# A transformer block with self and cross attention on one core: start-up memsets moved, the VectorE order of a pair of batches rearranged, cross queries ahead of the cross outputs

## What is computed

```
mod = silu(cond) @ W_mod + b_mod            # shift_a, scale_a, gate_a, shift_m, scale_m, gate_m
q, k, v = modulate(LN(x), shift_a, scale_a) @ W_qkv + b_qkv
x = x + gate_a * (softmax(q k' * 8**-0.5) v @ W_proj + b_proj)
q_c = LN(x) @ W_qc + b_qc ;  k_c, v_c = LN(context) @ W_kvc + b_kvc
x = x + (softmax(q_c k_c' * 8**-0.5) v_c @ W_cproj + b_cproj)
x = x + gate_m * (gelu(modulate(LN(x), shift_m, scale_m) @ W_mlp1 + b_mlp1) @ W_mlp2 + b_mlp2)
```

## Time and profile before

| | |
|---|---|
| median of 3 runs | 415.6 us (414.44, 415.6, 418.48) |
| the profiled execution | 415.69 us, its span 413.5 us |
| slots 4 to 13 (the loop) | about 95 to 270 us |
| slots 14 to 19 | about 270 to 345 us |
| MLP alone | from about 345 us |
| busy share of the span | PE 81%, ACT 66%, DVE 65%, POOL 46% |

### The profile page before, as it was taken

The page is one execution under the profiler, slowest core; times in us unless marked ns, Lnnn a source line. Parts: engine busy times, 40 slices in busy tenths (PEclk is TensorE's granted clock), DMA queues, the critical chain, the costliest instruction groups (busy, mean ns, idle before and its releaser), DMA issues.

```text
span 413.5 us, 15982 instructions
## 1 busy us (share of the span) xinstructions
PE 336.2 (81%) x5880; PEld 230.2 (56%) x5880; DVE 269.7 (65%) x682; ACT 272.3 (66%) x523; POOL 189.9 (46%) x462
## 2 busy tenths in 40 slices
PE   3455776978798898988989889899786487999994
PEld 2333454656676666766667666676554354445442
DVE  7764666868778788787888878877645350534311
ACT  1134563868688787787877888777682457577572
POOL 6523354756456565665656557555352310211200
PEclk9997998999999999999999999999998988999998
DMA  5323388243242523425243261433330300000101
GB/s 149 76 75 82 94 196 188 61 102 93 70 111 64 141 63 93 100 68 141 54 102 91 68 150 44 113 93 74 77 72 12 80 2 2 25 27 25 51 25 51
DMA packets 65548, 33.13 MB, mean 80 GB/s; under 512 B 8359, under 2 KB 65255, under 8 KB 65511
## 3 DMA queue, kind: packets, MB, share of 16 engines
q1 hardware_dynamic: 63599, 32.56, 32.3%
q10 hardware_dynamic: 1912, 0.07, 0.3%
HBM read 4.83 MB, written 2.10 MB: 17 GB/s over the span
## 4 chain that ended last, share of the span: by engine, by line
PE 40%; DVE 23%; issue 13%; SPq 10%; DMA 5%; ACT 3%; ACTq 2%; POOL 2%; DVEq 1%; POOLq 0%
SPq L406 7%; PE ps_o L1178 7%; PE wide L1170 7%; PE wide L1109 5%; PE ps_o L1131 5%; DVE mx L734 4%; DMA qkc_st<-qkcp 4%; DVE mxc L734 4%; DVE x_n L712 3%; PE ps_misc L1206 3%; PE wide L1120 2%; SPq L411 2%; DVE qkr L751 2%; PE ps_misc L1219 2%; DVE x_stats L696 2%
## 5 line engine op out<-in xcount | busy, mean ns | idle before, releaser
L734 DVE TENSOR_REDUCE mx<-wide 128x8 f32<-128x1024 f32 x64 | 78.0, 1219 | 26.4 <-PE wide L1109 26.4
L902 ACT ACTIVATE p_c<-wide 128x1024 f32<-128x1024 f32 x64 | 65.5, 1023 | 30.7 <-PE wide L1120 30.3
L902 ACT ACTIVATE p_s<-wide 128x1024 f32<-128x1024 f32 x64 | 65.5, 1023 | 19.7 <-PE wide L1120 19.0
L734 DVE TENSOR_REDUCE mxc<-wide 128x8 f32<-128x616 f32 x64 | 50.5, 789 | 21.7 <-PE wide L1109 21.7
L1131 PE MATMUL ps_o<-p_c,vc_m 128*32 128x128 f32 x1024 | 43.8, 292 | 0.3 <-ACT s_sum L923 0.2
L1131 PE MATMUL ps_o<-p_s,v_m 128*32 128x128 f32 x1024 | 42.5, 285 | 0.0
L523 POOL TENSOR_TENSOR x_ve<-x_mv,eps_sb 128x2 f32<-128x2 f32 x32 | 6.2, 195 | 76.5 <-DVE x_mv L703 76.5
L1109 PE MATMUL wide<-qkc_st 62*128 62x77 bf16 x512 | 20.5, 203 | 21.8 <-DMA qkc_st<-qkcp 11.3
L1109 PEld LDWEIGHTS wide<-qkc_st 62*128 62x128 bf16 x512 | 12.2, 98 | 36.4 <-DVE mxc L734 18.3
L1109 PE MATMUL wide<-qk_st 62*128 62x128 bf16 x512 | 26.0, 223 | 5.6 <-DVE mx L734 4.1
L1170 PE MATMUL wide<-m_nT,w_sb 128*128 128x512 f32 x64 | 30.0, 603 | 0.2 <-DVE mxc L734 0.2
(11 more groups left out here) (153 smaller groups left out, 811.8 us busy)
## 6 DMA issues: line engine op xcount, KB each, us to landing
qk_st<-qkp SPq DMA_DIRECT2D x96, 128.0 KB, 2.6
qkc_st<-qkcp SPq DMA_DIRECT2D x96, 128.0 KB, 2.5
out<-m_out SPq DMA_DIRECT2D x8, 256.0 KB, 2.3
xs<-x SPq DMA_DIRECT2D x3, 512.0 KB, 4.3
qk_st<-nmT SPq DMA_DIRECT2D x64, 4.0 KB
qkc_st<-nmcT SPq DMA_DIRECT2D x64, 4.0 KB
ctx_sb<-ctx SPq DMA_DIRECT2D x3, 308.0 KB
w_sb<-L_xcond_W_mlp SPq DMA_DIRECT2D x2, 256.0 KB, 4.8
```

The costliest lines, as they stand in the source:

```text
L734: nc.vector.reduce_max(mxt[:, b].rearrange("q (x r) -> q r x", r=2)[:, r], src, AX.X, negate=True).then_inc(sems[done], 1)
L902: nc.scalar.activation(dst[u % 2][:].rearrange("k x q -> k (x q)"), ps_st[:].rearrange("k s x -> k (s x)"), ACT.Exp, scale=SCALE).then_inc ...
```

## The change

Seven edits, none of which changes what is computed:

1. Start: the condition vector has a semaphore of its own (`cond_in`), so its transpose no longer waits for `w_mod`.
2. DVE's zeroing of `v_m` and the ones in it (`key_sums`) move from the head of the program and from beat 0 of slot -2 to the end of beat 5 of slot -2.
3. POOL's zeroing and ones of `qkc_st` and the zeroing of `qkcp` move from the end of slot -1 to the end of slot -2, behind a wait for `x_n_set`.
4. DVE: the two remainders `qkr` are apart: queries at beat 2 as before, keys at beat 3, after that beat's maxima. The statistics of the context move from beat 5 to beat 1, those of x1 from beat 4 to beat 5, the normalising of x from beat 6 to beat 5, and that of x1 at beat 6 from before the maxima to after them.
5. POOL: `split_max` of batch 1 of h comes before the self parts (`halves`) of a.
6. PE: `q_c` comes before `obc_t` at beat 7; `q_c` takes bank 0 and `obc_t` bank 1.
7. ACT: the copy `qcx` moves from beat 0 of the next slot, after `ocT`, to the end of beat 7, after the exponential.

```diff
--- before.py
+++ after.py
@@ -89,7 +89,7 @@
         ("max_s1", "here", 0), ("proj", "back1", 2),
         ("kv_c", "back1", 1),
         ("max_c0", "back2", 0), ("oc_t", "back3", 1), ("x1_t", "back1", 2),
-        ("obc_t", "back3", 0), ("q_c", "back1", 1), ("x_t", "far", 2)]
+        ("q_c", "back1", 0), ("obc_t", "back3", 1), ("x_t", "far", 2)]
 BANK = {name: bank for name, _, bank in MISC}
 
 
...
@@ -387,7 +387,7 @@
                 lo, hi = PIECES[n:n + 2]
                 sp.dma_start(ctx_sb[:, lo:hi], ctx[lo:hi].rearrange("b t c -> t b c")).then_inc(sems[f"c_in{n}"], 16)
 
-            sp.dma_start(cond_sb[:], cond).then_inc(sems["wm_in"], 16)
+            sp.dma_start(cond_sb[:], cond).then_inc(sems["cond_in"], 16)
             sp.dma_start(wmod_sb[:], w_mod).then_inc(sems["wm_in"], 16)
             load_x(0)
             sp.dma_start(wqkv_sb[:], w_qkv).then_inc(sems["wq_in"], 16)
@@ -585,14 +585,14 @@
                     split_max(h, 0, mx, nm, "mx_set", "nmh_set", "nm_set", "mts_ps")
                 if d:
                     gated(d)
+                if h:
+                    split_max(h, 1, mx, nm, "mx_set", "nmh_set", "nm_set", "mts_ps")
                 if a:
                     if not a.first():
                         q = a.shift(-1)
                         w(pool, f"qk_in{q.par}", 16 * NCMB * (q.turn + 1))
                     hold(pool, "qkr_set", a.n + 1)
                     halves(a, qkr[:], [qkp[:, :, n] for n in range(3)], "qk")
-                if h:
-                    split_max(h, 1, mx, nm, "mx_set", "nmh_set", "nm_set", "mts_ps")
                 if d:
                     rstd("x1", d)
                 if f:
@@ -604,6 +604,15 @@
                           kcr[:].rearrange("c (b k) -> c b k", b=G), "kvc0_set", "kc", "qkc_in")
                 if f:
                     split_max(f, 1, mxc, nmc, "mxc_set", "nmch_set", "nmc_set", "mtc_ps")
+                if far and far.first():
+                    pool.wait_ge(sems["x_n_set"], 1)
+                    for par in range(2):
+                        nc.gpsimd.memset(qkc_st[par][:, :, 1].bitcast(u32), 0).then_inc(sems["z_pool"], 1)
+                    nc.gpsimd.memset(qkcp[:].bitcast(u32), 0).then_inc(sems["pad_set"], 1)
+                    pool.wait_ge(sems["z_pool"], 8)
+                    for par in range(2):
+                        nc.gpsimd.memset(qkc_st[par][:, :, 1].rearrange("c m (b k) -> c m b k", b=G)[:, :, :, 0:S],
+                                         1.0).then_inc(sems["zk_set"], 1)
                 if a and a.first():
                     pool.wait_ge(sems["wc_in"], 16 * 2)
                     for n, src in ((2, wqc_sb), (3, wkvc_sb)):
@@ -612,13 +621,6 @@
                                 wdh[:, n, HALF * s_:HALF * (s_ + 1)].rearrange("c (d m) -> c d m", d=D),
                                 src[:, 0:C].rearrange("c (m s d) -> c s d m", s=2, d=D)[:, s_])
                         last.then_inc(sems["wdc_set"], 1)
-                    for par in range(2):
-                        nc.gpsimd.memset(qkc_st[par][:, :, 1].bitcast(u32), 0).then_inc(sems["z_pool"], 1)
-                    nc.gpsimd.memset(qkcp[:].bitcast(u32), 0).then_inc(sems["pad_set"], 1)
-                    pool.wait_ge(sems["z_pool"], 8)
-                    for par in range(2):
-                        nc.gpsimd.memset(qkc_st[par][:, :, 1].rearrange("c m (b k) -> c m b k", b=G)[:, :, :, 0:S],
-                                         1.0).then_inc(sems["zk_set"], 1)
 
             slots(pool, slot)
 
@@ -631,9 +633,6 @@
 
             for st in qk_st:
                 nc.vector.memset(st[:, :, 0].bitcast(u32), 0).then_inc(sems["zq_set"], 1)
-            for vt in v_m:
-                nc.vector.memset(vt[:], 0.0).then_inc(sems["z_dve"], 1)
-
             dve.wait_ge(sems["cond_t"], 1)
             nc.vector.tensor_copy(condT[:], ps_max[:, 0, 0:B]).then_inc(sems["condT_set"], 1)
             dve.wait_ge(sems["tanh_set"], 1)
@@ -802,8 +801,6 @@
                         residual(z, "projc_ps", "proj_c", "x2_set")
                     if t == 3 and d:
                         attention_out(d, "s", "o_t", "ot_ps", "rden_set", "o_set", "obt_ps")
-                    if t == 6 and d:
-                        normalise("x1", d, x_of(d), "x1t_ps")
                     if t == 7 and e:
                         attention_out(e, "c", "oc_t", "oct_ps", "rdenc_set", "oc_set", "obct_ps")
 
@@ -819,7 +816,6 @@
                         stats("x", far, x_of(far))
                         aggregate("x", far)
                         if far.first():
-                            key_sums()
                             tables(range(2), 1)
                             head_columns()
                     if t == 2 and a:
@@ -827,23 +823,30 @@
                         if not a.first():
                             w(dve, "qk2_set", a.n)
                         rest(ps_misc[BANK["qk"]][:, 0:GT], bdh[:, 0:1], qkp[:, 0, 0], qkr[:, 0])
+                    if t == 3 and a:
                         rest(ps_misc[BANK["qk"]][:, GT:2 * GT], bdh[:, 1:2], qkp[:, 1, 0],
                              qkr[:, 1]).then_inc(sems["qkr_set"], 1)
                     if t == 4 and d:
                         residual(d, "proj_ps", "proj", "x1_set")
+                    if t == 5 and d:
                         hold(dve, "x1_set", d.n + 1)
                         stats("x1", d, x_of(d))
                         aggregate("x1", d)
-                    if t == 5 and h:
+                    if t == 1 and h:
                         arrived("c_in", h, {0: (0,), 1: (1,), 3: (2, 3, 4)})
                         stats("ctx", h, ctx_of(h))
                         aggregate("ctx", h)
-                    if t == 6 and far:
+                    if t == 5 and far:
                         normalise("x", far, x_of(far), "xt_ps")
                         if far.first():
                             tables(range(2, 6), 2)
                             for st in qkc_st:
                                 nc.vector.memset(st[:, :, 0].bitcast(u32), 0).then_inc(sems["zq_set"], 1)
+                            for vt in v_m:
+                                nc.vector.memset(vt[:], 0.0).then_inc(sems["z_dve"], 1)
+                            key_sums()
+                    if t == 6 and d:
+                        normalise("x1", d, x_of(d), "x1t_ps")
                     if t == 7 and h:
                         normalise("ctx", h, ctx_of(h), "ctxt_ps")
                 if a and a.first():
@@ -972,14 +975,6 @@
 
                     if t == 0 and z:
                         copy(ocT[:], ps_misc[BANK["obc_t"]][:, 0:GT], "obct_ps", z, "ocT_set", "projc_ps")
-                    if t == 0 and f:
-                        w(act, "qc_ps", f.n + 1)
-                        if f.first():
-                            act.wait_ge(sems["bc_in"], 16 * 4)
-                        else:
-                            w(act, "qcr_set", f.n)
-                        nc.scalar.activation(qcx[:], ps_misc[BANK["q_c"]][:, 0:GT], ACT.Identity,
-                                             bias=bdh[:, 2:3]).then_inc(sems["qc0_set"], 1)
                     if t == 1 and e:
                         empty_max(e, 1, "max_c1", "mtc_ps", nmcT, "nmcT_set", "mc_in")
                     if t == 1 and a:
@@ -1052,6 +1047,14 @@
                         values(v_m[a.par], T, ps_misc[BANK["v"]][:, 0:G * C]).then_inc(sems["v_set"], 1)
                     if t == 5 and e:
                         sums(e, "c", ps_o, "pvc_ps", "sumc_set", "oct_ps")
+                    if t == 7 and d:
+                        w(act, "qc_ps", d.n + 1)
+                        if d.first():
+                            act.wait_ge(sems["bc_in"], 16 * 4)
+                        else:
+                            w(act, "qcr_set", d.n)
+                        nc.scalar.activation(qcx[:], ps_misc[BANK["q_c"]][:, 0:GT], ACT.Identity,
+                                             bias=bdh[:, 2:3]).then_inc(sems["qc0_set"], 1)
 
                 if a and a.first():
                     for n in range(4):
@@ -1083,9 +1086,10 @@
             mm, tr = nc.tensor.matmul, nc.tensor.transpose
 
             pe.wait_ge(sems["id_set"], 1)
-            pe.wait_ge(sems["wm_in"], 16 * 2)
+            pe.wait_ge(sems["cond_in"], 16)
             tr(ps_max[:, 0, 0:B], cond_sb[:], ident[0:B, 0:B]).then_inc(sems["cond_t"], 1)
             pe.wait_ge(sems["silu_set"], 1)
+            pe.wait_ge(sems["wm_in"], 16)
             for k in range(6):
                 last = mm(ps_max[:, int(k < 2), k * B:(k + 1) * B], wmod_sb[:, k * C:(k + 1) * C], siluT[:], start=True, stop=True)
                 if k in (1, 5):
@@ -1362,10 +1366,10 @@
                         flip_sums("oc_t", "c", e, "sumc_set", "oct_ps")
                     if t == 6 and d:
                         transposed("x1_t", "x1", d, T, "x1t_ps")
+                    if t == 7 and d:
```

(5 more changed lines are left out.)

## The result

The changed kernel takes **426.1 us** (median; 424.05 to 429.33), the kernel before, on the same chip, 415.1 (414.44 to 418.48): a ratio of 1.021, 95% interval [1.016, 1.027]. The forecast was 418.8 with a range to 422.5, so it is slower than forecast by 7 us, and outside the range. The profiled execution took 425.76 us, with a span of 424.0 against 413.5.

What follows compares the result with a forecast made beforehand. A ring of DVE and PE bounds the loop, but the edits lengthen a second chain (L533, SP, `nmT`) to its limit. Terms -2.2 + 3.6 + 0.6 + 1.0 + 0.1 = +3.1 on 415.69 gave 418.8 us, range 413 to 422.5.

Steps and rivals of the forecast that it cites:

- +0.06 us a slot, +0.6 us for ten slots: Loop: what DVE's holes and the earlier cross queries give, the queue of L533, SP and `nmT` takes back.
- the walk of the keys' remainder: Loop: L533 starts 2.3 us later, so `nmT` lands at 215.8, 0.55 us late; next slot at 218.3 against 218.26.
- The edits of `qcx` and of the banks I cost at nothing: Cross queries: POOL takes `qcx` 0.4 us sooner but SP waits for `nmcT`; `q_c` waits for ACT's reading of `max_c0`.
- start: Before slot 0: L677 ends at about 20.3 instead of 22.78 without POOL's memsets; a gain of 2.2 us taken.
- slots 0 and 1: No room on the chain through L533: its delay counts fully, +1.5 us in slot 0 and +1.9 in slot 1.
- slots 2 and 3: Slot 2's x1 transposes, behind the third cross maxima, add 0.2 us; slot 3 adds nothing, its cross stack's landing ending last.
- slot 14: Old second chain with SP busy: +1.5 us if its 1.80 us gap stays, +0.3 if taken up; +1.0 taken.
- slot 15 to the end of the span: Slots 15 to 17: cross queries 0.4 us earlier, x1 transposes 0.5 later, +0.1; the MLP is not touched.
- The 19.0 that the prediction worked out for L677: Start: by the skill's shared-port rule L677 should have slipped in after the first memset, at about 19.0.
- the queue which I had taken for the limit: Loop: POOL's late L533, SP's stack issues and the landing of `nmT` end the slot, next slot at 218.3.
- The slower rival: Loop: POOL's `rstd` of x1 ahead of the first cross maxima's casts; 0.3 us more a slot, 421.8 us, chance 0.20.
- The other two rivals: Loop: queue has room, slot 17.1, 414.9 us, chance 0.20; DVE's holes filled fully, slot 16.9, 411.7 us, chance 0.15.

Runs made afterwards that it cites:

- the run with start and cross queries alone: Kernel before plus only the start edits and the cross queries ahead of the cross outputs, with their bank numbers: 17.08 us a slot, 411.9 us, ratio 0.984.
- the kernel with the keys back: Changed kernel with both halves of the remainders at beat 2 and POOL's second self-maxima casts behind the halves again: 17.36 us a slot, 416.4 us, ratio 0.999.
- the kernel before with x1 late: Kernel before with only x1's statistics behind the second cross maxima and its normalising behind the third: 17.74 us in most slots, 423.1 us, ratio 1.015.
- the run with other banks: Changed kernel with only bank numbers of small jobs changed (`qk` to 2, `ctx_t` to 1, among others): 17.42 us a slot, 422.0 us, ratio 1.009.

## Why the prediction was wrong

**The step that failed is the loop's "+0.06 us a slot, +0.6 us for ten slots"**; measured were 0.68 us a slot, +6.1 in all. In the walk of the keys' remainder I followed one of the two that wait for `qkr_set`, POOL's L533. The other one is PE's next job in bank 0, `ctx_t`; its wait was put at nothing, without a reason. Of banks the prediction asked only where `q_c` moves ("The edits of `qcx` and of the banks I cost at nothing", which held: the run with start and cross queries alone has them and got faster), and not who waits for a bank whose release comes later. By first maxima, against the forecast:

| stretch | forecast | measured |
|---|---|---|
| start (slot 0 begins at 25.83 instead of 27.84) | -2.2 | -2.0 |
| slots 0 and 1 | +3.4 | +4.7 |
| slots 2 and 3 | +0.2 | -0.5 |
| slots 4 to 13 | +0.6 | +6.1 |
| slot 14 | +1.0 | +0.7 |
| slot 15 to the end of the span | +0.1 | +1.5 |
| sum | +3.1 | +10.5 |

- *Start.* Right in size, and L677's instruction answered at once. The two x_n of pair 1, though, fared differently (view of the tile in that stretch: shortest, median and longest in ns):

```profile
L711 DVE TENSOR_SCALAR x_n<-xs,x_mv,x_rstd x2: 609/960/1312, 16.9 to 17.5; 128x128 f32<-128x128 f32 x2
```

  The first came through as L533 ended, at 17.5, as the 0.94 us of the earlier trace rows had let me assume for both. The second began within 0.1 us of L535 and ended at 18.78, 0.1 us after it. The Trainium skill (SBUF — State Buffer, Who interferes with whom) has whoever issues first keep the shared ports for the whole instruction. The first x_n agrees with that; for the second the two starts are too close to say; L677 before does not agree, since it was held over five memsets. The 19.0 that the prediction worked out for L677 by this rule is late besides: it was asked at 17.87, ahead of the first memset at 18.08.
- *Slots 0 and 1.* The mechanism was right, the size was not: they took 2.3 and 2.5 us more (18.09 and 18.01 against 15.82 and 15.54) for a forecast of 1.5 and 1.9. Against the kernel with the keys back it is 1.77 and 1.61, so 0.5 and 0.9 us are common to both (16.32 and 16.40 there). In slot 0 the edits did not bring them: the kernel before with x1 late, whose slot 0 is that of the kernel before, took 16.31. At its end the context's transposes and the next scores took PE 0.62 and 0.54 us, and 0.37 each in the kernel before. In slot 1 L533 began 9.0 us after the first maxima (52.92 against 43.92), where the forecast had 8.1 and the kernel before 6.2: the third maxima already came 4.5 us into it, 3.7 before. PE's granted clock over that slot was 0.97 in the changed kernel, 0.79 with the keys back and 1.00 before; what made it longer is not explained further.
- *Slots 2 and 3.* The forecast had the landing of a cross stack end last in both, the first one 1.2 us later than 68.45. In the changed kernel neither slot has a landing on its chain of waits; it runs through L533 and POOL instead, and the two slots took 0.5 us less than before, not 0.2 more.
- *The loop.* The changes add up slot by slot: cross queries -0.33 (17.41 to 17.08; the forecast had 0.45), x's normalising and the context's statistics early -0.08 (to 17.00), x1 late +0.36 (to 17.36), keys late +0.73 (to 18.09). The forecast had the gain of the first in it, about rightly; the last two were wrong or missing. Late keys cost 0.73 with x1 early or late (17.00 to 17.73, 17.36 to 18.09) and on the kernel before (17.41 to 18.14). With the bank out of the way 0.41 of it stays when x1 is early (17.00 to 17.41), and that is the queue which I had taken for the limit; the bank alone is then worth 0.32 (17.73 to 17.41), and 0.67 when x1 is late (18.09 to 17.42). Its walk was right to 0.1 us; it just was not what came last.
- *The slower rival* was at work (the row L1228 above), a slot of 17.36 by itself. It was priced at 0.3 us beyond the queue's limit, and measured 0.36 against a kernel that has no such limit. With the bank out of the way it and the late keys together gave 17.42, about the forecast's slot, and not 18.1. The other two rivals, under 17.2, fell with the first row of waits.
- *The end.* The drain and the MLP took 1.5 us more, 0.95 of it by the last cross maxima (334.81 - 287.06 = 47.75 us into the drain before, 344.76 - 296.06 = 48.70 now). The granted clock does not tell why: over the drain it is 0.93 in both (stretch, its length, PE's busy time with its instructions, granted clock, DMA share, GB/s; first before). The cause stays open.

```profile
287.06:335.60 48.54, 34.73 (x744) 0.93 0.22 52
```

```profile
296.06:345.60 49.54, 34.42 (x744) 0.93 0.22 51
```

The wait for the bank could be known beforehand. The list of jobs has `ctx_t` behind `qk` in bank 0, and `qkr_set` frees it. The transposes of the context fill columns 0 to 153 of the bank and the late half reads columns 256 to 511, so no data stand in each other's way; the program's semaphores guard whole banks, and whoever reads a bank late holds all of it. The Trainium skill (PSUM — Partial Sum Buffer, Summary: rules for kernel authors) says to read PSUM from a different bank, or at least a different quadrant, while a matmul runs, and to guard by bank with semaphores. No run here tried it without the guard; the wait that it made is the 0.67 us a slot that the run with other banks gave back.

## What to carry to other kernels

When an instruction is moved later, list everyone who waits for its semaphore, and of the releases of buffers and banks above all: the one who pays may use none of its data. A reading of PSUM that goes behind other work should stand in a bank that the other engine does not need next. And the same swap of two steps on one queue can gain or cost, by what a third engine's queue holds behind them: 0.28 us gained, 1.1 lost.

## What the runs showed of the hardware

In the profiled execution of the kernel before with x1 late, the longest of its five (426.9 us against a median of 423.1), three slots of the loop took 19.3 to 19.9 us instead of 17.74. PE's clock in one of them (slot 7, 151.6 to 170.9; columns as above) and its timeline there:

```profile
167.00:169.00 2.00, 2.00 (x32) 0.50 0.01 2
169.00:171.00 2.00, 2.00 (x25) 0.69 0.01 2
```

```profile
164.98 0.23 PE L1225 MATMUL ps_misc<-ident,nmc 128*32 128x128 bf16 x1 [0.74 <-POOL nmc L558]
...
166.41 0.41 PE L1199 MATMUL ps_misc<-ident,x_n 128*128 128x128 f32 x2 [0.62 <-DVE x_n L712]
...
167.51 1.08 PE L1132 MATMUL ps_o<-p_s,v_m 128*32 128x128 f32 x16
```

PE was idle for 0.74 us and, after 0.8 us of work, for 0.62; then the granted clock fell to 0.50, the 1.2 GHz level, for some 3 us, and the product by the values took 1.08 us where it takes 0.64 at the full one. The slot was 1.6 us longer. In the next slot the same two gaps were 0.77 and 0.37 us and the clock stayed at 1.00. But the gaps alone do not decide it. Slot 11 of the same execution has them as long as slot 7, to 0.02 us, and kept its clock:

```profile
225.65:243.41 17.76, 15.80 (x358) 1.00 0.38 90
```

```profile
239.02 0.23 PE L1225 MATMUL ps_misc<-ident,nmc 128*32 128x128 bf16 x1 [0.74 <-POOL nmc L558]
...
240.43 0.41 PE L1199 MATMUL ps_misc<-ident,x_n 128*128 128x128 f32 x2 [0.60 <-DVE x_n L712]
```

Slot 13 (0.73 and 0.61 us) kept it as well. So two short waits close together can be followed by a slower clock, at a price of 1.6 us, and need not be; what decides is not shown. The changed kernel had its gaps of 1.02 and 0.73 us some 6 us apart, and kept its clock at 1.00 from 97 to 270 us.
